# Causal attention inside a one-core adaLN block: scores laid out with keys on partitions, the row maxima taken in a pass of their own ahead of time

## What is computed

```python
# L0_attn_ref: b=1, seq=2048, HID=256, H=16, Q_LORA=96, KV_LORA=64, D_NOPE=128, D_ROPE=64
q = _rms_norm(x @ w_qa, q_a_norm_w) @ w_qb                     # per head 128 plain + 64 rotary
kv = x @ w_kva
c_kv, k_rope = (kv[..., :KV_LORA], kv[..., KV_LORA:])
kv_up = _rms_norm(c_kv, kv_a_norm_w) @ w_kvb
q_rope = _apply_rope(q_rope, cos, sin)
scores = jnp.einsum('bhsd,bhtd->bhst', q_full, k_full) * scale
scores = jnp.where(mask[None, None], scores, jnp.finfo(scores.dtype).min)   # causal
attn = jax.nn.softmax(scores, axis=-1)
out = jnp.einsum('bhst,bhtd->bhsd', attn, v)
return out.transpose(0, 2, 1, 3).reshape(b, seq, H * D_V) @ w_o
```

## Time and profile before

| | |
|---|---|
| median of three runs | 1441.09 us (1438.73 to 1442.52) |
| span of the profiled execution | 1433.7 us |
| PE busy | 1257.6 us, 88% of the span |
| DVE, ACT, POOL busy | 1066.8, 847.4, 508.8 us |
| part `attend` up to its first transposes | until 138.7 us |
| eight turns | about 1028 us, 128.4 us each |
| after `attend` | from about 1166 us |

### The profile page before, as it was taken

One profiled execution on the slowest core, in us unless ns is written; L12 is line 12 of the kernel. 1 busy time (PEld: TensorE's weight loads), 2 busy tenths in 40 slices (PEclk: granted clock), 3 DMA queues, 4 the chain that ended last, 5 costly groups with the idle time before them and its releaser, 6 DMA issues. The chain is left out here.

```text
span 1433.7 us, 34876 instructions
## 1 busy us (share of the span) xinstructions
PE 1257.6 (88%) x10712; PEld 1091.1 (76%) x10712; DVE 1066.8 (74%) x2241; ACT 847.4 (59%) x2213; POOL 508.8 (35%) x509
## 2 busy tenths in 40 slices
PE   1765999899989999998998999899899977989897
PEld 1654787788878787887877787788778766878786
DVE  1634888688878868886886888688788877676676
ACT  0254776677767767776766776677767753232232
POOL 0122444444434444543444444434534452111100
PEclk9977999999999999999999999999999988999999
DMA  9400000000000000000000000000000040000000
GB/s 278 114 0 9 3 10 2 4 2 10 3 3 2 10 4 2 10 2 4 2 10 3 2 10 2 4 1 10 4 2 3 9 133 15 1 16 0 15 5 25
DMA packets 23728, 26.56 MB, mean 19 GB/s; under 512 B 5825, under 2 KB 22849, under 8 KB 23105
## 3 DMA queue, kind: packets, MB, share of 16 engines
q1 hardware_dynamic: 16848, 17.74, 3.9%
q10 hardware_dynamic: 6672, 6.29, 1.9%
HBM read 19.28 MB, written 4.75 MB: 17 GB/s over the span
## 5 line engine op out<-in xcount | busy, mean ns | idle before, releaser
L705 POOL TENSOR_TENSOR pt_lo<-pt 128x512 f16<-128x512 f32 (+3 forms) x387 | 357.1, 939 | 575.6 <-ACT pt L747 555.6
L747 ACT ACTIVATE pt<-bank 128x512 f32<-128x512 f32 (+3 forms) x515 | 264.6, 537 | 267.0 <-PE bank L886 242.2
L738 ACT ACTIVATE probs<-bank,nmx 128x512 f32<-128x512 f32 (+3 forms) x648 | 397.5, 626 | 37.4 <-DVE nmx L803 34.2
L796 DVE TENSOR_REDUCE mx<-bank 128x1 f32<-128x512 f32 (+3 forms) x584 | 342.3, 617 | 54.3 <-PE bank L875 51.5
L886 PE MATMUL bank<-ident,probs 128*128 128x128 f32 x2189 | 322.4, 280 | 17.6 <-ACT probs L738 11.0
L886 PEld LDWEIGHTS bank<-ident,probs 128*128 128x128 f32 x2189 | 236.9, 142 | 33.2 <-issue 15.8
L817 DVE TENSOR_TENSOR pt_lo<-pt 128x512 f16<-128x512 f32 (+3 forms) x257 | 195.3, 760 | 76.2 <-ACT pt L747 76.2
L899 PE MATMUL bank<-values,pt 128*128 128x128 f16 x2176 | 236.8, 220 | 13.1 <-POOL pt_lo L705 9.8
L900 PE MATMUL bank<-values,pt_lo 128*128 128x64 f16 x2176 | 226.4, 193 | 0.0
L899 PEld LDWEIGHTS bank<-values,pt 128*128 128x128 bf16 x2176 | 194.5, 98 | 21.7 <-POOL pt_lo L705 12.2
L900 PEld LDWEIGHTS bank<-values,pt_lo 128*128 128x128 f16 x2176 | 189.7, 98 | 3.3
(11 more groups left out here) (180 smaller groups left out, 2062.1 us busy)
## 6 DMA issues: line engine op xcount, KB each, us to landing
xs<-in_L_attn_x ACTq DMA_DIRECT2D x1, 2048.0 KB, 24.0
lat<-in_L_attn_w_o SPq DMA_DIRECT2D x1, 2048.0 KB, 25.7
xs_again<-in_L_attn_x SPq DMA_DIRECT2D x1, 2048.0 KB, 7.8
out<-xs_again SPq DMA_DIRECT2D x4, 512.0 KB, 2.8
lat<-in_L_wmod SPq DMA_DIRECT2D x1, 1536.0 KB, 16.0
wq_pair_hi<-wq_parts SPq DMA_DIRECT2D x9, 144.0 KB, 2.2
wq_pair_lo<-wq_parts SPq DMA_DIRECT2D x9, 144.0 KB, 2.2
lat<-in_L_attn_w_qb SPq DMA_DIRECT2D x1, 1152.0 KB, 7.9
```

The source lines that it names most:

```text
L705: pool.tensor_tensor(out=pt_lo[:, s % PT_RING, 0:n], in0=full, in1=cut(full), op=ALU.subtract).then_inc(low_ok["p"], 1)
L738: act.activation(probs[:, s % P_RING, 0:n * P], s_bank[s % S_RING][:, 0:n * P], ACT.Exp, bias=nmx[:, item % MX_RING:item % MX_RING + 1], a ...
L747: act.activation(pt[:, s % PT_RING, 0:n * P], bank_of(u)[:, 0:n * P], ACT.Copy, scale=P_SCALE).then_inc(bank_read["a"], 1)
L796: dve.tensor_reduce(out=mx[:, slot, c:c + 1], in_=of, axis=AXX, op=ALU.max).then_inc(chunk_max, 1)
```

## The change

The scores are now formed with keys on partitions, so what leaves the exponential is already in the layout that the product with the values needs, and nothing is transposed. The work of a turn is cut into 40 units (`UNITS`): one unit is 256 keys (two halves of 128) by 512 queries of one head. Full units lie below the diagonal (24 in a turn), diagonal units come in two kinds, with 512 and 384 live columns in their halves or with 256 and 128 (8 each).

Since the maximum of a query is no longer along the free axis, it is taken ahead: `maximum` forms the high-by-high product alone in the old layout, one chunk of up to 512 keys by 128 queries at a time (80 in a turn, `LEAD` = 24 chunks ahead of the units), and DVE reduces it. Per item (now 512 queries of one head, 8 in a turn) DVE builds the negated maxima as diagonals (`spread`), a product with ones brings them to all partitions (`shift_rows`), ACT copies them to `shift`, and before each unit ACT (or DVE for the small diagonal units) writes `shift` into the two PSUM banks of the unit (`seed`). The score products add onto that, and ACT takes the exponential of 128x1024 at once with no bias and no row sum. The row sum comes from a column of ones behind the values (129 and 65 columns instead of 128 and 64). POOL alone forms `pt_lo`. DVE adds the halves of the result for two query tiles at once (`evacuate`). The tables for the rotation are no longer held whole; SP loads a quarter before each query group, and the four loads of them in `prepare` are gone. The last turn is written out apart and leaves out what looks ahead of it.

```diff
+GROUPS = (3, 2, 1, 0)
+ITEMS = [(g, h) for g in GROUPS for h in range(2)]
+    UNITS += [(_k, 2 * _n, None) for _n in range(2 * _g)] + [(_k, BT * _g, 0), (_k, BT * _g + 2, 2)]
+PT_RING, SHIFTS = 4, 4
+LEAD = 24
+PREP = {2: 5, 3: 13, 4: 20, 5: 31}
+def chunks_at(r):
+    return (2 * r + LEAD, 2 * r + LEAD + 1)
+SHIFT_ROUND = {i: (last_chunk(i) - LEAD) // 2 + 1 for i in range(1, NI + 1)}
...
-                for half in range(2):
-                    act.dma_start(k["cos2"][half * DR:half * DR + DR, :], k["cos_t"]).then_inc(ld_rope, 16)
-                    act.dma_start(k["sin2"][half * DR:half * DR + DR, :], k["sin_t"]).then_inc(ld_rope, 16)
...
+                def low_parts(hp, u):
+                    at = pt_slot(u)
+                    if UNITS[u % NU][2] is None:
+                        pool.wait_ge(exp_done, ops_value(hp, u))
+                        full = pt[:, at].rearrange("p a n -> p (a n)")
+                        pool.tensor_tensor(out=pt_lo[:, at].rearrange("p a n -> p (a n)"), in0=full, in1=cut(full),
+                                           op=ALU.subtract).then_inc(low_ok, 1)
...
+                def seed(hp, u):
...
+                    if u >= 2:
+                        act.wait_ge(exp_done, ops_value(hp, u - 2))
+                    act.activation(s_pair[u % 2][:, :, :], shift[:, item % SHIFTS:item % SHIFTS + 1, :].to_broadcast([P, 2, BW]),
+                                   ACT.Copy).then_inc(seeded["a"], 1)
+                def exponentials(hp, u):
+                    at = pt_slot(u)
+                    act.wait_ge(pv_done, hp * NU + (CREDIT + u - PT_RING + 1))
+                    if UNITS[u % NU][2] is None:
+                        act.wait_ge(s_done, hp * (2 * NU) + (S_CREDIT + 2 * u + 2))
+                        act.activation(pt[:, at], s_pair[u % 2][:, :, :], ACT.Exp).then_inc(exp_done, 1)
...
+                def maximum(hp, c, last=False):
...
+                    wait_seen(pe, hp, w - 2)
+                    last = pe.matmul(to[:, 0:cols], q_hi[:, g, h, t * P:t * P + P], kt_hi[h][:, part * BW:part * BW + cols],
+                                     start=True, stop=not diagonal)
...
+                def scores(hp, u, half):
+                    if half == 0:
+                        e = "v" if seed_on_vector(u) else "a"
+                        pe.wait_ge(seeded[e], seed_value(e, hp, u))
+                    for m, (a, b) in enumerate(((0, 0), (0, 1), (1, 0))):
+                        last = pe.matmul(to, keys[a], q[b], start=False, stop=(m == 2 and d is None), skip_group_check=True)
...
+                def weigh(hp, u, half):
+                    pe.wait_ge(low_ok, ops_value(hp, u) - (0 if d is None or half else 1))
...
+                        for half in range(2):
+                            if not (last and r >= NU):
+                                scores(hp, r, half)
+                            if not (last and two[half] >= NC + SPARE):
+                                maximum(hp, two[half], last)
+                            weigh(hp, r - 2, half)
...
-                for n, tiles in enumerate((slice(0, BT), slice(BT, NT))):
-                    dve.tensor_reduce(out=rden[:, tiles, :], in_=rowsum[:, tiles, 0:H, :], axis=AXX, op=ALU.add).then_inc(den_ok, 1)
```

More of the change, by code:

```diff
@@ L720, in _ @@
+                for u in range(2):
+                    low_parts(0, u)
+                with pool.Fori(0, NP - 1) as hp:
+                    turn(hp, False)
+                turn(NP - 1, True)
             @block.scalar
             def _(act):
[L722 to L727 removed]
@@ new lines, in _ @@
+                for e in (0, 1):
+                    for part in range(2):
+                        query_plain(0, e, part)
+                    for hd in range(2):
+                        query_high(0, e, hd)
+                act.wait_ge(opened, 1)
+                shift_rows(0, 0)
+                seed(0, 0)
+                seed(0, 1)
+                for u in range(2):
+                    exponentials(0, u)
+                    seed(0, u + 2)
+                with act.Fori(0, NP - 1) as hp:
+                    turn(hp, False)
@@ new lines, in _ @@
+                pe.wait_ge(consts_ok, 1)
+                for pair in s_pair:
+                    for half in range(2):
+                        last = pe.matmul(pair[:, half, :], ones_r[:, :], kt_hi[0][:, 0:BW], start=True, stop=True)
+                last.then_inc(opened, 1)
+                for e in (0, 1):
+                    for part in range(3):
+                        query_products(0, e, part)
+                for c in range(chunks_at(2)[0]):
+                    maximum(0, c)
+                    if c == FIRST_SHIFT_AFTER:
+                        shift_rows(0, 0)
@@ L926, in cut @@
+                for u in range(2):
+                    for half in range(2):
+                        scores(0, u, half)
+                with pe.Fori(0, NP - 1) as hp:
+                    turn(hp, False)
+                turn(NP - 1, True)
 def cut(a):
```

685 lines of the change are left out of this document (361 added, 324 removed).

## The result

The changed kernel takes **1507.6 us** (median of 4 runs, 1504.6 to 1513.3) where the kernel before takes 1440.8 on the same chip: ratio 1.048, 95% interval 1.045 to 1.051 (the quotient of the two medians is 1.046, inside the interval). Forecast were 1353 us and a chance of 0.11 for slower.

A forecast was written before the change was run, and what follows sets the result against it. PE was taken as the bound: 109.0 us of work, 5.2 of waits and 3.0 at the loop's edge made a 117.2 us turn, 11.2 less; with +2 once, span 1346, median 1353 us. Range 1308 to 1415.

The forecast's parts named there:

- The ring of exponential, seed and scores: Reuse of a unit's two PSUM banks: 2.5 us needed against 3.3 of PE work, slack 0.8 us a round.
- seeds into PSUM are slow: Rival: ACT's seed writes at twice the price bound the turn at 129 us, 1448 us, up to 1600; chance 0.07.
- 129 and 65 columns are slow: Rival: odd column counts in value products read slower, up to twice 0.085 us a pair, 1535 us; chance 0.05.
- DVE's latest round: Round where query sum, spread and result move meet on DVE: PE was to wait about 0.5 us a turn.
- 8x0.25: PE's waits for the result's move at the next item: eight places a turn at 0 to 0.5 us each.
- 4x0.5: Waits in the four rounds a turn where ACT has `q_hi` copies and POOL `q_lo` on top: 0.5 us each.
- PE's work: Sum of PE's matmul prices in a turn: 109.0 us after the change, 5.7 less than before.
- The waits to be gained: Kernel before: 13.7 of a turn's 128.4 us taken as not work, 3.0 at the edge and 10.7 of waits.
- The clock: PE's granted clock in the turns, 0.99 before; below 0.97 was named as a sign of being wrong.
- Once in the program: Outside the turns: -6 at ACT's queue, +18 before first value products, -7 last turn, -3 in `experts`; sum +2 us.
- The ring is tighter: Rival: each round loses 0.1 to 0.25 us in the bank cycle, turn 121 to 127, about 1400 us; chance 0.20.
- The waits all but vanish: Rival: only the loop's edge remains as wait, turn 112 us, 1312 us in total; chance 0.17.

The follow-up runs named there:

- e4: Changed kernel with POOL forming only the first 128 of 1,024 columns of full units' low parts (work left out): 1426.7 us, ratio 0.994.
- e1: Changed kernel with DVE's seed and result move placed straight behind the two maxima of a round: 1473.3 us, ratio 1.026.
- e12: Changed kernel with each DVE maximum read over the first 128 columns only (work left out): 1466.8 us, ratio 1.020.
- e9: Changed kernel with DVE's seed and result move behind the maxima and the query sums on POOL, spread left on DVE: 1439.0 us, ratio 0.999.
- e13: As e10, with a query group's work on POOL laid over three rounds, one head a round: 1394.5 us, ratio 0.970.
- e11: As e9, with the second query group's rotation tables loaded at the start into free slots of `shift`: 1436.6 us, ratio 0.998.
- e5: Changed kernel with the edits of e1 and e4 together: 1397.7 us, ratio 0.972.
- e8: Changed kernel with the order of e1 and both query sums and spreads on POOL: 1524.7 us, ratio 1.060.
- e2: Changed kernel with query groups started at rounds 7, 15, 21, 31 so that no sum meets a spread: 1509.3 us, ratio 1.051.
- e15: Changed kernel with the order of e1, sums on POOL one head a round, spread on ACT, second group's tables early: 1375.8 us, ratio 0.957.
- e3: Changed kernel with DVE's spread as four `tensor_scalar` of 128 columns instead of one `tensor_tensor`: 1603.1 us, ratio 1.115.
- e14: As e9, with the spread moved from DVE to ACT as four 128-column copies with a scale: 1400.8 us, ratio 0.974.
- e10: As e9, with an item's last maximum and spread ahead of the round's query products on DVE: 1436.6 us, ratio 0.998.

## Why the prediction was wrong

By parts (before the first value product, to the last, behind it) the forecast was 155.6 + 923.5 + 267.0 = 1346 of span; measured are 162.7 + 1070.8 + 269.0 = 1502.5. So 147 of the 156 us lie in the turns.

- **Right: what ACT and POOL do, and the busy times.** Busy times of ACT 84 (88 said), POOL 82 (81), DVE 89 (86), exponential and seed 1.02 and 1.03 (1.04 and 1.07). The ring of exponential, seed and scores holds PE up once a turn, at the loop's edge (8 waits, 15.9 us), and nowhere else in the changed kernel. The rivals "seeds into PSUM are slow" and "129 and 65 columns are slow" are excluded by rows: a seed 1028 ns, a value pair 0.089 us from start to start.
- **The step that failed: "DVE's latest round (...) has 4.3 us of work against 2.3 to 2.7 of PE, less 1.4 that the two work banks absorb: about 0.5".** It is 4.9 to 5.1. Two things in it were wrong. The price: the earlier trace rows gave 0.81 for a sum beside a POOL that was busy 55 us a turn with instructions of 1.09 us; that was a mean of undisturbed sums of 0.69 and held ones of up to 1.42. The change makes POOL's instructions 1.95 us, and the sum costs 1.28, the spread 1.34. e4 shows it. And the place: what is queued last is the result's move, for which PE waits with its value products; the work banks cushion only maxima. e1 shows it. DVE's load has a share in the loss (e12, 41 us), but a small one in these waits (73.3 to 61.9 us).
- **"8x0.25"** for the moves of the items sized 2 us; with that round all waits before L1007 are 10.7 us a turn. **"4x0.5"** for the four rounds with `q_hi` and `q_lo` found nothing: PE waited for low parts 0.8 us in the whole run. Such waits came up only when the sums stood in the same rounds of POOL (e9), and went with thin rounds (e13). The shift product's 3.8 us a turn and the maxima's 2.7 were no terms at all. In sum 18.2 us of waits stand against 5.2: +13.0.
- **PE's work** is 113.4 us and not 109.0: +4.4. A value pair with a column more in each product takes 0.089 instead of 0.085 (272 of them, 1.1 us), and the middle step of a product of 512 columns is 0.235 and not 0.23 (about 1 us). The largest part is a switch that was not counted: 32 of the 80 maxima in a turn stand behind a mask, which like a value product has 16-bit operands, and the first product of fp32 operands behind it takes 0.32 us at 512 columns instead of 0.24, about 0.08 more each, 2.7 us a turn. One of either kind (the changed kernel, each with the product behind it):

```profile
639.21 0.48 PE L964 MATMUL bank<-kt_b_hi,q_hi 128*128 128x512 f32 x1
639.53 0.23 PE L1007 MATMUL bank<-values,pt 128*128 128x129 f16 x1
...
642.58 0.39 PE L964 MATMUL bank<-kt_b_hi,q_hi 128*128 128x512 f32 x1
642.81 0.23 PE L1007 MATMUL bank<-values,pt 128*128 128x129 f16 x1
```

- **The waits to be gained** were fewer than the prediction took. Its 10.7 us a turn in the kernel before are what was left over from its price list; the idle times of PE in the timeline of one such turn, 470.2 to 598.6, add up to about 8 us, with the edge's 2.95 in them, where the changed kernel's turn has 17.1.
- **The clock** was no term, only named as a sign of being wrong (below 0.97); it is 0.97 in this turn, which costs 2 to 3 us, and 0.95 in the next ones on either side. The edge is 2.5 instead of 3.0. 117.2 + 13.0 + 4.4 - 0.5 + 2.3 = 136.4, the turn measured.
- **Once in the program:** the -6 at ACT's queue is right (first query product at 115.8 against 121.8), the rest of the start is +25 instead of +18: a wait of 5.5 us before the second group, in part for its tables (e11), and half clock behind it. The end is -1 instead of -3.
- **The rivals.** "The ring is tighter" was nearest in kind, a turn made longer by waits, with 121 to 127 a turn and only 0.20. But its reason, the ring, was not what happened, and its bound was set by slack of engines; none of its rows asked how late one queued instruction can get. The two rivals whose times reach 1507.6 (slow seeds, 1448 to 1600, and odd column counts, up to 1535) are the ones that the rows exclude, so that their figures came near is chance. "The waits all but vanish" had PE's weight loads for it; they did fall, from 103.4 to 89.8 us a turn, and the turn grew by 8.1 us.

**What is shown and what is not.** It is shown that sum and spread stand still beside POOL (each single duration, e4), that the order carries part of the wait (e1, e5), that DVE's load carries another part (e12), and that POOL's waits come from a burst in its queue at equal load (e8, e13). What half clock costs by itself was not isolated. In the turns of the table every run with a wait of 4.6 us or more has a clock of 0.95 or less or, once, 0.97, and the others 0.99 or 1.00, save e1 and e2 at 0.95, whose longest are 3.0 and 3.5. Of e15's 6.6 us of gaps, 2.3 are the loop's edge. e3's whole loss of 96 us was read from its rows and not tested further.

## What to carry to other kernels

When work moves from a shared to a single engine, ask of each instruction that somebody waits for what stands before it in its queue in the worst round, and price that block with the new length of the neighbour's instructions: balance over a turn (DVE 65% busy here) says nothing of it. Ask of a row's mean what its shortest and longest are: 812 ns was 689 with some of 1417. An SBUF-to-SBUF instruction of DVE of the two kinds seen here costs up to one whole instruction of POOL more beside it; put it on ACT (e14) or put what is waited for ahead of it (e1). Lay bursts over several rounds: that gave 2.7% (e13 against e10), at the same load.

## What the runs showed of the hardware that was not expected

- DVE's SBUF-to-SBUF instructions are not slowed in proportion but held: 0.69 alone, up to 2.37 us beside a POOL instruction of 1.89, and done 0.54 to 0.61 us after the end of POOL's, whenever they start in it; mean 1.28 and 1.34, back to 0.75 and 0.86 when POOL's are short. Four pieces of 0.29 came to 0.63 each. DVE instructions with PSUM on one side stayed within 30 ns of each other at each shape in the turns (maxima of 512 columns 670 to 694, seeds 682 to 697), and ACT's SBUF-to-SBUF copies of 128 columns within 384 to 403 (e14).
- After a standstill of 5 us PE's granted clock was 0.54 for the next 3.5 us. Shorter waits can do it too, but not each time: in e15 a wait of 2.2 us was followed by a clock of 0.63 from 400.5 to 404.5, and one of 2.1 at 763.9 was not, with 1.00 in the whole turn; e5's six waits of about 2.6 us left it at 1.00.
- The first product of fp32 operands with 512 columns behind one with 16-bit operands takes about 0.08 us longer to the next start than behind another fp32 one (0.32 against 0.24), behind a mask as behind a value product.
- Value products with 129 and 65 columns at rows of 130 values cost 0.089 us a pair, against 0.085 with 128 and 64.
